# Leaky ReLU of the first convolution read from PSUM by VectorE, depthwise steps moved out of that stage, and x transposed from the token tile

## The reference

```python
# L0, for each image (xe: tokens x channels)
q, k, v = split(batchnorm(xe) @ w_qkv + b_qkv)          # q, k without their channel mean
q2, k2 = l2n(q*q / sum_c(q*q)), l2n(k*k / sum_c(k*k))   # normed over channels / over tokens
attn = (v + q2 @ (k2.T @ v) / sqrt(4096)) @ w_ln + b_ln
y = leaky_relu(conv1x1(concat(attn, x), w1) + b1, 0.2)  # 96 -> 96 channels
y = leaky_relu(conv3x3(y, w2) + b2, 0.2)                # 96 -> 96 channels
x = conv1x1(y, w3) + b3 + x
# L1 (and L3): relu, depthwise 3x3, pointwise 48 -> 48, batch norm
# L2: mixture of 4 experts by the image's mean: expand 48 -> 192, relu,
#     depthwise 3x3 on 192 channels, relu, project 192 -> 48, plus its input
```

## Time and profile before

| | |
|---|---|
| runs of the kernel before | 1320.14 us median of 3 (1319.85 to 1320.87) |
| the profiled execution | 1316.4 us, its span 1314.6 us |
| mean granted TensorE clock | 0.95 of full |
| PE busy | 1194.1 us (91%) |
| DVE busy | 874.0 us (66%) |
| ACT busy | 537.0 us (41%) |
| POOL busy | 150.9 us (11%) |

### The profile page before, as it was taken

One profiled execution on the slowest core, in us unless ns is written; L12 is line 12 of the kernel. 1 busy time (PEld: TensorE's weight loads), 2 busy tenths in 40 slices (PEclk: granted clock), 3 DMA queues, 4 the chain that ended last, 5 costly groups with the idle time before them and its releaser, 6 DMA issues.

```text
span 1314.6 us, 14707 instructions
## 1 busy us (share of the span) xinstructions
PE 1194.1 (91%) x4981; PEld 767.6 (58%) x4981; DVE 874.0 (66%) x1090; ACT 537.0 (41%) x876; POOL 150.9 (11%) x72
## 2 busy tenths in 40 slices
PE   3799888999899998999899998999899998999995
PEld 2565565657565675656566574656656574655533
DVE  5542469954698269965598358974699458982760
ACT  2411435334722545235632446335542447233431
POOL 0400023000400014000400004000310004000000
PEclk9789869999999998999989998999989998999997
DMA  3201710099103960089202980069301980049106
GB/s 61 45 14 29 96 29 0 1 118 133 33 0 41 137 105 0 0 101 134 47 0 37 121 125 0 0 80 141 61 0 19 126 123 14 0 64 129 42 17 89
DMA packets 200077, 76.07 MB, mean 58 GB/s; under 512 B 191245, under 2 KB 191858, under 8 KB 200050
## 3 DMA queue, kind: packets, MB, share of 16 engines
q1 hardware_dynamic: 200050, 75.73, 41.3%
HBM read 13.65 MB, written 6.29 MB: 15 GB/s over the span
## 4 chain that ended last, share of the span: by engine, by line
PE 54%; issue 18%; POOL 8%; SPq 8%; DVE 4%; ACT 3%; DMA 3%; POOLq 0%; DVEq 0%; ACTq 0%
PE bank L1080 33%; POOL y_parts L958 7%; PE bank L1104 4%; PE bank L1091 3%; SPq L832 3%; SPq L857 3%; PE bank L1022 3%; PE bank L1148 2%; DMA y_parts<-a_parts 2%; PE bank L1171 2%; PE bank L1170 2%; POOL tok L953 2%; SPq L853 1%; PE bank L1107 1%; PE bank L1106 1%
## 5 line engine op out<-in xcount | busy, mean ns | idle before, releaser
L1080 PE MATMUL bank<-y_parts,w_h 96*96 96x512 f32 x1152 | 313.6, 423 | 4.6 <-ACT y_parts L1310 4.6
L629 DVE SCALAR_TENSOR_TENSOR dwa<-h1a,dyn,dwa 128x1024 f32<-128x1024 f32 x240 | 294.3, 1274 | 0.0
L1080 PEld LDWEIGHTS bank<-y_parts,w_h 96*96 96x96 f32 x1152 | 192.8, 168 | 108.3 <-issue 14.5
L629 DVE SCALAR_TENSOR_TENSOR dwb<-h1b,dyn,dwb 128x1024 f32<-128x1024 f32 x128 | 155.8, 1275 | 0.0
L1080 PE MATMUL bank<-y_parts,w_l 96*96 96x512 f32 x576 | 154.9, 415 | 0.0
L958 POOL TENSOR_TENSOR y_parts<-y,y_parts 96x512 fp32r<-96x512 f32 x56 | 127.6, 2299 | 193.1 <-ACT y_parts L1310 193.0
L1104 PE MATMUL bank<-a_parts,wt_h 128*96 128x512 f32 x384 | 119.5, 420 | 15.0 <-DMA y_parts<-a_parts 15.0
L1080 PEld LDWEIGHTS bank<-y_parts,w_l 96*96 96x96 f32 x576 | 98.7, 171 | 47.9 <-issue 0.3
L953 POOL TENSOR_TENSOR tok<-tok,u 128x1536 f32<-128x1536 f32 x8 | 22.4, 2798 | 763.3 <-DVE u L570 763.3
L667 DVE SCALAR_TENSOR_TENSOR y<-y 96x512 f32<-96x512 f32 x64 | 90.1, 1408 | 26.9 <-ACT y L1296 25.9
L708 DVE SCALAR_TENSOR_TENSOR a_parts<-v,a_parts 96x512 fp32r<-96x512 f32 x64 | 44.0, 687 | 85.8 <-ACT a_parts L1359 83.0
(11 more groups left out here) (223 smaller groups left out, 1718.2 us busy)
## 6 DMA issues: line engine op xcount, KB each, us to landing
y_parts<-a_parts SPq DMA_DIRECT2D x32, 396.0 KB, 6.1
y_parts<-a_parts SPq DMA_DIRECT2D x64, 192.0 KB, 6.6
a_parts<-a_parts SPq DMA_DIRECT2D x32, 264.0 KB, 3.3
dwa<-in_x_dram SPq DMA_DIRECT2D x64, 96.0 KB, 2.9
tok<-in_x_dram SPq DMA_DIRECT2D x64, 96.0 KB, 4.2
...
```

Source lines behind the costliest of these rows:

```text
L629: nc.vector.scalar_tensor_tensor(out=dst, in0=tap_input(n, t), scalar=weight, in1=dst, op0=ALU.mult, op1=ALU.add).then_inc(tap_step, 1)
L1080: last = nc.tensor.matmul(bank[0:C2, :], wgt[:, t, :], src[:, rows, cols], start=t + n == 0, stop=t == TAPS - 1 and n == 2)
```

## The change

Four things change together.

- **conv1 output.** ACT's copy of the bank is scaled by 0.2 (`y1_slope`). DVE then takes two maxima of the bank and that copy: the first writes `y1_h`, rounded and reordered, from the bank read at the same 128-element step (`bank_tokens`) and `y1_tokens`; the second writes `y1` in place. ACT's reordered copy (L1310) is gone. The bank is free after the second maximum, not after ACT's copy. DVE waits for the end of its first maximum before it issues the second, and POOL's subtraction waits for both.
- **depthwise steps.** The four steps of the conv1 stage leave it. conv2 keeps 40, which are now the steps 1 to 40, and the places after it have 2, 1, 3 and 4 instead of 1, 1, 1 and 3.
- **order on DVE after conv2.** The last w3 output and the last low part of L1 come ahead of the first low part of L3.
- **x.** `load_xa` and its 8 DMAs go. `load_x` has 12 DMAs instead of 8: four put a second copy of the even rows' x into the q columns of the token tile's second half, so that 96 columns in a row hold x as the transposes want it. It stands first in SP's iteration, and the transposes read `tok`. At the start of the program the w2 weights now stand behind 12 such DMAs, not 16.

```diff
@@ -266,7 +266,7 @@
                       + [(h1b_ready, 6, n + 3) for n in range(4)] + [(h1a_ready, 8, n + 1) for n in range(8)])
         C_1, C_2 = 0, 8
-        ring_c = Ring(banks[4:6], [(y1_linear, CHUNKS, n + 1) for n in range(CHUNKS)]
+        ring_c = Ring(banks[4:6], [(y1_max, CHUNKS, n + 1) for n in range(CHUNKS)]
                       + [(y2_ready, CHUNKS, n + 1) for n in range(CHUNKS)])
...
@@ -285,7 +285,7 @@
         BY_CONV1, BY_CONV2, BY_PROJECT = 0, CHUNKS, 2 * CHUNKS
-        steps_at = (0, 1, 1, 1, 0, 1, 0, 0) + (8, 5, 5, 5, 5, 4, 4, 4) + (1, 1, 1, 3)
+        steps_at = (0,) * CHUNKS + (8, 5, 5, 5, 5, 4, 4, 4) + (2, 1, 3, 4)
         assert sum(steps_at) == TAP_STEPS
         def unit(n):
...
@@ -390,6 +390,9 @@
         def y1_tokens(k):
             return columns(y1[:, :, :], (k % Y1_BUFFERS) * BANK, [[WQ, PAIRS], [1, WQ], [128, 4]])
+
+        def bank_tokens(bank):
+            return columns(bank, 0, [[WQ, PAIRS], [1, WQ], [128, 4]])
         def y1_view(tile, k):
...
@@ -662,11 +665,13 @@
                     if k < 1 or image is None:
                         continue
                     depthwise_at(f, BY_CONV1 + k - 1)
-                    dve.wait_ge(y1_linear, CHUNKS * image + k)
-                    buffer = (k - 1) % Y1_BUFFERS
-                    nc.vector.scalar_tensor_tensor(out=y1[:, buffer, :], in0=y1[:, buffer, :], scalar=SLOPE,
-                                                   in1=y1[:, buffer, :], op0=ALU.mult, op1=ALU.max).then_inc(y1_max, 1)
+                    dve.wait_ge(y1_slope, CHUNKS * image + k)
+                    bank, buffer = ring_c.bank(C_1 + k - 1)[0:C2, :], (k - 1) % Y1_BUFFERS
+                    nc.vector.tensor_tensor(y1_view(y1_h, k - 1), bank_tokens(bank), y1_tokens(k - 1), ALU.max).then_inc(y1h_ready, 1)
+                    dve.wait_ge(y1h_ready, CHUNKS * image + k)
+                    nc.vector.tensor_tensor(y1[:, buffer, :], bank, y1[:, buffer, :], ALU.max).then_inc(y1_max, 1)
                 if image is not None:
+                    dve.wait_ge(y1_max, CHUNKS * image + CHUNKS)
                     dve.wait_ge(y1h_ready, CHUNKS * image + CHUNKS)
                     nc.vector.tensor_tensor(y1_view(y1_l, CHUNKS - 1), y1_tokens(CHUNKS - 1),
                                             y1_view(y1_h, CHUNKS - 1).bitcast(F32), ALU.subtract).then_inc(y1l_last, 1)
...
@@ -764,13 +769,12 @@
             def iteration(f, attn, back):
                 conv2_out(f, back)
                 depthwise_at(back, BY_PROJECT)
+                w3_out(f, PCHUNKS - 1)
+                depthwise_at(back, BY_PROJECT + 1)
+                l1_low_part(f, PCHUNKS - 1)
                 if back is not None:
                     l3_low_part(back, 0)
-                depthwise_at(back, BY_PROJECT + 1)
-                w3_out(f, PCHUNKS - 1)
-                depthwise_at(back, BY_PROJECT + 2)
-                l1_low_part(f, PCHUNKS - 1)
-                if back is not None:
+                    depthwise_at(back, BY_PROJECT + 2)
                     l3_low_part(back, 1)
                     depthwise_at(back, BY_PROJECT + 3)
                 else:
...
@@ -822,15 +826,6 @@
         def x_rows(image):
             return a["x"][image].rearrange("(j b) (q i) c -> b q j i c", b=2, q=WQ)
-        def load_xa(sp, image, projected):
-
-            src = x_rows(image)
-            wait(sp, project_done, projected)
-            by_column = xa.rearrange("p (i b c) -> p b i c", b=2, c=C)
-            for n in range(2 * WQ):
-                par, q = n % 2, n // 2
-                sp.dma_start(by_column[q::WQ, par], src[par, q]).then_inc(xa_loaded, 16)
-
         def load_x(sp, image):
             src = x_rows(image)
...
@@ -838,6 +833,8 @@
             for n in range(2 * WQ):
                 par, q = n % 2, n // 2
                 sp.dma_start(tok[q::WQ, par, :, X_AT:X_AT + C], src[par, q]).then_inc(x_loaded, 16)
+            for q in range(WQ):
+                sp.dma_start(tok[q::WQ, 1, :, Q_AT:Q_AT + C], src[0, q]).then_inc(x_loaded, 16)
         def copy_beside(sp, n, half):
             r0, rows = half * PAIRS // 2, PAIRS // 2
...
@@ -916,13 +908,11 @@
                         sp.dma_start(to, frm).then_inc(wt_placed, 16)
             def iteration(f, attn, back):
-                beside_l1(sp, f)
-                if attn is not None and back is not None:
-                    load_xa(sp, attn, PCHUNKS * (f - 1) + 2)
-                if back is not None:
-                    beside_l3(sp, back, f + 1)
                 if attn is not None:
                     load_x(sp, attn)
+                beside_l1(sp, f)
+                if back is not None:
+                    beside_l3(sp, back, f + 1)
                 copy_x2(sp, f)
                 if back is not None:
                     store(sp, back)
...
@@ -955,6 +945,7 @@
             def split_y1(image):
                 for k in range(POOL_CHUNKS):
                     pool.wait_ge(y1h_ready, CHUNKS * image + k + 1)
+                    pool.wait_ge(y1_max, CHUNKS * image + k + 1)
                     nc.gpsimd.tensor_tensor(y1_view(y1_l, k), y1_tokens(k), y1_view(y1_h, k).bitcast(F32),
                                             ALU.subtract).then_inc(y1l_ready, 1)
...
@@ -1003,12 +994,12 @@
                 for n in chunks:
                     if n == 0:
-                        pe.wait_ge(xa_loaded, 32 * WQ * (image + 1))
+                        pe.wait_ge(x_loaded, 16 * X_LOADS * (image + 1))
                     bank = ring_a.take(pe, image, A_XT + n)
                     for m in range(4):
                         i = 4 * n + m
                         last = nc.tensor.transpose(bank[0:C2, m * 128:(m + 1) * 128],
-                                                   xa[:, i * C2:(i + 1) * C2], ident[:, :])
+                                                   token(1, i, Q_AT, C2), ident[:, :])
                     last.then_inc(xt_done, 1)
             def attention_scores(image):
...
@@ -1293,21 +1283,11 @@
                             act.wait_ge(y1l_ready, POOL_CHUNKS * image + k - Y1_BUFFERS)
                         else:
                             after(act, y1l_last, image)
-                        nc.scalar.activation(y1[:, (k - 1) % Y1_BUFFERS, :], ring_c.bank(C_1 + k - 1)[0:C2, :], ACT.Copy)\
-                            .then_inc(y1_linear, 1)
-                    if image is not None and k > 1:
-                        y1_high_part(image, k - 2)
-                    for i, n in enumerate(expand_beside[k] if f is not None else ()):
+                        nc.scalar.activation(y1[:, (k - 1) % Y1_BUFFERS, :], ring_c.bank(C_1 + k - 1)[0:C2, :], ACT.Copy, scale=SLOPE)\
+                            .then_inc(y1_slope, 1)
+                    for n in expand_beside[k] if f is not None else ():
                         if n >= 4:
                             h1a_rows(f, n)
-                        if k == CHUNKS and i == 0 and image is not None:
-                            y1_high_part(image, CHUNKS - 1)
-                if f is None:
-                    y1_high_part(image, CHUNKS - 1)
-
-            def y1_high_part(image, k):
-                act.wait_ge(y1_max, CHUNKS * image + k + 1)
-                nc.scalar.activation(y1_view(y1_h, k), y1_tokens(k), ACT.Copy).then_inc(y1h_ready, 1)
             def first_tap(image, n):
                 _, dst, c, _ = unit(n)
```

More of the change, by code:

```diff
@@ L918, in iteration @@
             def iteration(f, attn, back):
+                if attn is not None:
+                    load_x(sp, attn)
                 beside_l1(sp, f)
-                if attn is not None and back is not None:
-                    load_xa(sp, attn, PCHUNKS * (f - 1) + 2)
                 if back is not None:
                     beside_l3(sp, back, f + 1)
-                if attn is not None:
-                    load_x(sp, attn)
                 copy_x2(sp, f)
@@ L1028, in attention_sums @@
                 bank = ring_a.take(pe, image, A_G)
-                pe.wait_ge(x_loaded, 32 * WQ * (image + 1))
                 pe.wait_ge(k_scaled, image + 1)
@@ L1279, in root_of_k, with conv1_slope @@
                 nc.scalar.activation(rk[:, :], rk[:, :], ACT.Sqrt, scale=float(TOKENS)).then_inc(root_k, 1)
-            def conv1_high(image, f):
+            def conv1_slope(image, f):
                 for k in range(BEFORE, CHUNKS + 1):
```

16 lines of the change are left out of this document (6 added, 10 removed).

## The result

The changed kernel takes 1266.4 us, the median of 4 runs (1264.8 to 1268.1); the kernel before took 1320.0 in 4 runs beside it (1317.6 to 1320.9). The ratio is 0.9603, with a 95% interval from 0.9582 to 0.9625. The forecast was 1271 us, so it lies 5 us too high. In the profiled executions the span is now 1264.3 us, 50.3 less than before.

The account below looks back on a forecast made before the run. The prediction took ACT's 2.55 us a chunk to pace the conv1 stage, with PE waiting and its clock falling. Gains of 28.0, 19.8 and 1.9 less 0.5 give 49.2 us: 1320.14 to 1271 us, range 1256 to 1297.

Parts of the forecast that it names:

- gain from conv2's start to T: From conv2 to T: 3.2 us from the clock, 1.4 from x, less 1.3 for late depthwise steps; 3.3 us.
- gain up to image 0's conv2: Start: first transposes 1 us later for more DMAs, image 0's stage gains 0.5; together 0.5 us lost.
- sum of the gains: Whole kernel: 28.0 from seven stages, 19.8 from six iterations to T, 1.9 from iteration 7, less 0.5; 49.2 us.
- The stage: conv1 stage: DVE's two maxima set a pace of 1.98 us a chunk instead of ACT's 2.55; 4.0 us a stage.
- No stretch beside POOL: conv1 stage: the new maxima, each with one SBUF input, are not lengthened while POOL works; 1.26 and 0.75 us.
- POOL: conv1 stage: POOL's subtraction needs 1.70 us with handing over.
- The clock: End of stage and conv2: fuller PE keeps 2.4 GHz, so conv2's first 81 products get back 3.2 us.
- The depthwise steps: After conv2: four moved steps make project 2 wait 1.2 us for a ReLU; they take 1.3 us of the gain.
- 1.4 from x: Before T: PE's wait for the load of x goes, since the load is issued some 70 us before; 1.4 us.
- The strides add up: Rival, conv1 stage: first maximum 1.80 us, pace 2.52, no stage gain, clock falls too; 1320 us, chance 0.10.
- held up by POOL: Rival, conv1 stage: maxima stretched beside POOL as L667 is, pace 2.71, conv2 1.9 us later; 1333 us, chance 0.08.
- Iteration 7: Last iteration: gain of 1.9 us from conv2's start to its project 2.

Follow-up runs that it names:

- e11: Against e5: y kept in the tokens' order, so only PSUM is read at a step; 1250.5 us.
- e9: Changed kernel with the first maximum reading the bank in contiguous order, y still at its step (columns mismatched); 1265.9 us.
- e10: Changed kernel with the first maximum reading y in contiguous order, the bank still at its step (columns mismatched); 1258.9 us, a single run.
- e7: Changed kernel with the second maximum taken from two SBUF inputs instead of the bank and y1; 1296.6 us.
- e4: Kernel before with only the depthwise steps moved and DVE's order after conv2 changed; 1314.3 us.
- e6: Kernel before with repeated conv1 products and expansions, same output, to keep PE busy in the stage; 1324.8 us.
- e3: Kernel before with only the new load and transposes of x; 1308.9 us.
- X: The part of the change with the load and transposes of x; alone against the kernel before, 1308.9 us.
- M: The part of the change with the two maxima; alone against the kernel before, 1296.9 us.
- e8: Changed kernel with the depthwise steps and DVE's order put back, so the two maxima and the new x only; 1291.7 us.
- S: The part of the change with the depthwise steps and DVE's order after conv2; alone against the kernel before, 1314.3 us.
- e2: Changed kernel with x loaded and transposed as before the change; 1264.4 us.
- e5: Against e2: one depthwise step moved, last four places 3, 1, 2, 4 instead of 2, 1, 3, 4; 1258.6 us.
- e1: Kernel before with the two maxima alone, depthwise steps and x as before; 1296.9 us.

## Why the prediction was right, point by point

| term, us | predicted | measured |
|---|---|---|
| gain in the conv1 stage, each of 7 | 4.0 | 4.7 (19.09 to 14.37) |
| gain from conv2's start to T, each of 6 | 3.3 | 3.0 (85.57 to 82.60) |
| length of an iteration | 142.6 | 142.24 |
| gain up to image 0's conv2 | -0.5 | 0.2 (69.67 to 69.43) |
| gain in iteration 7 and the tail | 1.9 | 0.25 (206.70 to 206.45) |
| sum of the gains | 49.2 | 50.3 of the span |

The terms sum to 51.3 by the measured sizes. The difference to 50.3 lies mostly in the loop's first iteration of the kernel before. It took 148.54 us, 1.4 less than the one I read, so the iterations there do not all repeat each other to within 0.3 us. It gave 6.35 (142.19 now), and the six of the loop gave 45.1 together, 7.5 each (209.41 to 1107.90 before, 204.43 to 1057.85 after). Iteration 0 gave 4.7.

Of the 5 us by which the forecast is too high, only 1.1 are the sum. Most of the rest is the 3.7 by which the median of the kernel before lay above its profiled execution, and which I carried over: the changed kernel's median lies 0.3 above its profiled one (1266.1).

- *The stage.* The mechanism was right; the mis-sized term is the first maximum, priced at 1.26 and measured at 1.07. My bounds, 1.12 to 1.25 for one SBUF input with the step, were read from L697 and L671. L671's counterpart takes 1.10 now, and 0.72 in e11 with y in order, so the step of y accounts for its excess, and the bank's step adds none (e9, e10). With 1.07 DVE's pace would be 1.79; the loop over two banks, which I had at 1.9 and which with 1.07 in the same sum comes to 1.8, holds it at 1.86.
- *No stretch beside POOL.* Right: all 64 second maxima take 0.69 (e7 shows what the bank input avoids). What I did not see is the other direction. I took L667's stretch as the cost of L667's own inputs. e4 shows that a good part of it was made by the depthwise steps, which held up POOL.
- *POOL* at 1.73 for 1.70: right.
- *The clock.* Right: 3.1 for 3.2. e6 shows it alone with 2.96. That PE's gaps decide it is an incomplete account: e3 has much the same gaps as the kernel before and a far shorter stretch of low clock.
- *The depthwise steps.* The wait of 1.09 before project 2 was forecast as 1.2. L1 starts at 66.3 for 65.6, because its first weight load waits for the copies beside L1:

```profile
697.41 0.48 PEld L1094 LDWEIGHTS bank<-a_parts,wt_h 128*96 128x96 f32 x3 [0.95 <-DMA y_parts<-a_parts]
```

SP issues the first of them 54.7 us after conv2's start (685.83), where I had 55.4, and 11.6 us lie between that and L1, where I had 10.2, read from the end of the transfers in a window. Project 2 starts at 74.7 for 74.3: DVE's idle 1.24 us ahead of the w3 output was not in my ledger. So T comes at 82.6 for 82.3.
- *x.* Here a step failed. "1.4 from x" is a gain of X only on the kernel before or with M (e3, e8). With S in the kernel the old load comes in time, since its DMAs go out earlier, as e2 shows and e5 too, where project 2 does not wait. So T comes at the same time without X, and the 1.4 in the sum is no gain of the new load. The number came out all the same, because the wait for x ends with S alone. X even costs something at the start: in the changed kernel the first transposes wait 2.9 us for x, in e2 for no DMA, and image 0's conv2 starts 0.8 us later (69.43 for 68.59), in e3 1.3 later than before and in e8 1.9 later than in e1. Single runs of equal code differ there by up to 1.6 (before and e4), so the size is uncertain.
- *The strides add up* and *held up by POOL* fell, by e9, e10 and the 64 second maxima. The Trainium skill, SBUF — State Buffer, section "Specifications (TRN2)", gives a penalty for each new line of 16 bytes in SBUF and 8 in PSUM; it stands in this section, not in the one that the prediction names for it. The 0.36 us for y agree with the SBUF half. For DVE and ACT reading a bank no run shows the PSUM half: 0.71 and 0.59 at a step of 512 bytes.
- *Iteration 7* came to project 2 1.4 us sooner, where I had 1.9 (76.27 to 74.84 after conv2's start), and gave 1.2 of it back where PE waits for the copies beside L3: 1.99 us now (L1094 at 1151.72), before 0.74 (L1104 at 1201.92).
